# The inverse roots of the query and key norms: from GpSimd's power to ten Vector operations in PSUM

## The reference, cut to what matters

```
for i in range(6):
    x = attn_layer(shift_tokens(x), ...) + x
    x = ffn_layer(shift_tokens(x), ...) + x

# in attn_layer: 16 heads of 64
q, k, v = split(x @ Wqkv, 3)
l2norm(t) = t / maximum(norm(t, axis=-1), 1e-12)
q = l2norm(q) * q_scale ; k = l2norm(k) * k_scale
q = q * cos * scale + rotate_half(q) * sin * scale      # k: 1 / scale
out = local_attention(q, k, v) @ Wo                     # windows of 32, each sees 64 keys
```

## Time and profile before

| | us |
|---|---|
| median of 3 runs | 4746.68 (4745.28 to 4752.33) |
| the profiled execution | 4743.42 |
| its span in the trace | 4741.6 |

### The profile page before, as it was taken

How to read it: one execution, slowest core, us unless ns; L and a number is a source line. 1 busy time by engine, 2 the same in 40 slices (tenths; PEclk the granted TensorE clock), 3 DMA queues, 4 the chain that set the end, 5 groups by cost and what they waited for, 6 DMA issues and landing times. The chain is left out here.

```text
span 4741.6 us, 161504 instructions
## 1 busy us (share of the span) xinstructions
PE 4145.7 (87%) x67078; PEld 2784.5 (59%) x67078; DVE 2917.3 (62%) x4217; ACT 2627.4 (55%) x4417; POOL 3317.3 (70%) x1514
## 2 busy tenths in 40 slices
PE   5878788779999999999999999999999999999994
PEld 2434344356666666666666666666666666666663
DVE  5565656556666666666666666666666666666664
ACT  2535354446556556666556555656566555655562
POOL 0000000189889888988888889988898888888891
PEclk8989888899999999999999999999999999999997
DMA  0000000112222222222222222222222222222222
GB/s 27 2 15 2 15 16 2 41 45 56 65 70 74 54 69 65 71 56 65 65 69 63 56 65 73 75 51 69 65 72 57 62 65 69 63 56 65 69 73 71
DMA packets 284546, 258.84 MB, mean 55 GB/s; under 512 B 122871, under 2 KB 258508, under 8 KB 271148
## 3 DMA queue, kind: packets, MB, share of 16 engines
q1 hardware_dynamic: 283820, 248.14, 19.5%
HBM read 117.63 MB, written 29.77 MB: 31 GB/s over the span
## 5 line engine op out<-in xcount | busy, mean ns | idle before, releaser
L783 DVE TENSOR_TENSOR products<-bank_d,table 128x1024 f32<-128x1024 f32 x772 | 937.9, 1215 | 722.5 <-ACT sq L610 696.5
L908 POOL TENSOR_TENSOR rnorm<-clamped,minus_half 128x32 f32<-128x32 f32 x192 | 1044.0, 5438 | 16.0
L903 POOL TENSOR_TENSOR products<-products 128x2048 f32<-128x2048 f32 x192 | 870.7, 4535 | 152.0 <-DVE products L783 152.0
L409 PE MATMUL bank_d<-w_qkv,xT 128*128 128x512 f32 x1544 | 806.4, 625 | 19.6 <-DVE products L783 14.7
L610 ACT ACTIVATE sq<-bank_d 128x512 f32<-128x512 f32 x772 | 467.9, 606 | 478.7 <-PE bank_d L409 468.6
L926 POOL TENSOR_TENSOR qk_rot<-products,rnorm 128x2048 f32<-128x2048 f32 x192 | 695.5, 3622 | 14.9 <-POOL rnorm L908 14.5
L870 POOL MEMSET ident<- 128x128 f32 x1 | 0.2, 205 | 917.1 <-POOLq L1044 917.1
L781 DVE TENSOR_REDUCE ss<-sq 128x16 f32<-128x1024 f32 x386 | 468.6, 1214 | 232.5 <-ACT sq L610 232.5
L933 POOL TENSOR_TENSOR prob<-prob,inv_sum 128x1024 f32<-128x1024 f32 x192 | 365.1, 1901 | 187.5 <-DVE inv_sum L763 187.5
L1471 DVE TENSOR_REDUCE part_max<-s_max 128x1 f32<-128x512 f32 (+3 forms) x768 | 398.5, 554 | 151.2 <-PE s_max L1220 100.5
L455 PE MATMUL bank_a<-ident,qk_rot 128*128 128x128 f32 x3072 | 414.7, 291 | 76.8 <-issue 64.7
(11 more groups left out here) (158 smaller groups left out, 7216.9 us busy)
## 6 DMA issues: line engine op xcount, KB each, us to landing
v_back<-v SPq DMA_DIRECT2D x96, 768.0 KB, 5.4
w_qkv<-in_Wqkv_dram SPq DMA_DIRECT2D x25, 1024.0 KB, 5.1
v_back<-v SPq DMA_DIRECT2D x192, 128.0 KB, 5.4
w_qkv<-in_Wqkv_dram SPq DMA_DIRECT2D x25, 512.0 KB, 5.4
xs<-x_layers SPq DMA_DIRECT2D x194, 64.0 KB, 2.1
w_o<-in_Wo_dram SPq DMA_DIRECT2D x24, 512.0 KB, 5.5
xr<-x_layers SPq DMA_DIRECT2D x96, 128.0 KB, 2.2
x<-x SPq DMA_DIRECT2D x96, 128.0 KB, 1.8
```

The lines of the kernel that those rows point to most:

```text
L409: nc.tensor.matmul(bank[:, :], xT[:, P * a:P * (a + 1)], w_qkv[:, col:col + 512], start=True, stop=True).then_inc(d_filled if i < 8 else a ...
L783: nc.vector.tensor_tensor(products[:, a, head:head + 8, :, :].rearrange("p h r (o d) -> p h r o d", o=2), bank[:, :].rearrange("p (h r d) ...
L903: link(nc.gpsimd.tensor_tensor(products[:, a, :, 0, :], products[:, a, :, 0, :], products[:, a, :, 1, :], ALU.add))
L908: link(nc.gpsimd.tensor_tensor(rnorm[:, a, :], clamped[:, a, :], minus_half[:, :], ALU.pow))
```

## The change

`inverse_norms` leaves POOL. DVE computes the 32 inverse roots of a half right behind the product of that half's last chunk (chunk 3 and chunk 7): the clamped sum of squares, a first guess by integer arithmetic on the bits, one cubic correction, one Newton step. Nine linked operations and a last one, each 128x32. Their intermediate values x, t, u lie in the PSUM bank of that last product, so the bank is freed (`d_free`) by the last root and not by the product. The product counts in a new semaphore, `products_ready`, on which POOL's `add_products` starts; `norm_qk` now waits on `d_free` for the roots.

```diff
--- before.py
+++ after.py
@@ -168,8 +168,9 @@
 
         ss = sb("ss", [P, 2, 2 * HEADS])
         rnorm = sb("rnorm", [P, 2, 2 * HEADS])
-        clamped = sb("clamped", [P, 2, 2 * HEADS])
-        minus_half = sb("minus_half", [P, 2 * HEADS])
+        root_y = sb("root_y", [P, 2 * HEADS])
+        root_u = sb("root_u", [P, 2 * HEADS])
+        minus_half = sb("minus_half", [P, 2])
         epsilon = sb("epsilon", [P, 2])
         var_eps = sb("var_eps", [P, 2])
         rstd = sb("rstd", [P, 2])
@@ -222,6 +223,7 @@
         a_filled, a_free = sem("a_filled"), sem("a_free")
         squared = sem("squared")
         var_ready = sem("var_ready")
+        products_ready = sem("products_ready")
         qk_ready = sem("qk_ready")
         table_ready = sem("table_ready")
         scores_ready, scores_used = sem("scores_ready"), sem("scores_used")
@@ -780,11 +782,32 @@
                 if c:
                     nc.vector.tensor_reduce(ss[:, a, HEADS * kq:HEADS * (kq + 1)], sq[i // 2 % 2][:, :, :], AX.X, ALU.add)
                 head = HEADS * kq + 8 * c
-                nc.vector.tensor_tensor(
+                product = nc.vector.tensor_tensor(
                     products[:, a, head:head + 8, :, :].rearrange("p h r (o d) -> p h r o d", o=2),
                     bank[:, :].rearrange("p (h r d) -> p h r d", r=2, d=DH // 2).unsqueeze(3).to_broadcast([P, 8, 2, 2, DH // 2]),
                     t4[:, kq, :, :].rearrange("p (r o) d -> p r o d", o=2).unsqueeze(1).to_broadcast([P, 8, 2, 2, DH // 2]),
-                    ALU.mult).then_inc(d_free, 1)
+                    ALU.mult)
+                if i % 4 == 3:
+                    product.then_inc(products_ready, 1)
+                    dve.wait_ge(products_ready, 2 * pair.n + a + 1)
+                    inverse_norms(a, bank).then_inc(d_free, 1)
+                else:
+                    product.then_inc(d_free, 1)
+
+            def inverse_norms(a, bank):
+
+                x, t, u = (bank[:, 2 * HEADS * k:2 * HEADS * (k + 1)] for k in range(3))
+                y, w = root_y[:, :], root_u[:, :]
+                link(nc.vector.tensor_scalar(x, ss[:, a, :], FLT_MAX, 1e-24, ALU.min, ALU.max))
+                link(nc.vector.tensor_scalar(y.bitcast(i32), x.bitcast(i32), -0.5, float(RSQRT_MAGIC), ALU.mult, ALU.add))
+                link(nc.vector.tensor_tensor(t, x, y, ALU.mult))
+                link(nc.vector.tensor_tensor(t, t, y, ALU.mult))
+                link(nc.vector.tensor_scalar(w, t, 0.375, -1.25, ALU.mult, ALU.add))
+                link(nc.vector.tensor_tensor(u, t, w, ALU.mult))
+                link(nc.vector.scalar_tensor_tensor(y, u, 1.875, y, ALU.add, ALU.mult))
+                link(nc.vector.tensor_tensor(t, x, y, ALU.mult))
+                link(nc.vector.scalar_tensor_tensor(t, t, -0.5, y, ALU.mult, ALU.mult))
+                return nc.vector.scalar_tensor_tensor(rnorm[:, a, :], t, 1.5, y, ALU.add, ALU.mult)
 
             def variances(s):
 
@@ -902,17 +925,12 @@
             def add_products(s, a):
                 link(nc.gpsimd.tensor_tensor(products[:, a, :, 0, :], products[:, a, :, 0, :], products[:, a, :, 1, :], ALU.add))
 
-            def inverse_norms(a):
-
-                link(nc.gpsimd.tensor_scalar(clamped[:, a, :], ss[:, a, :], FLT_MAX, 1e-24, ALU.min, ALU.max))
-                link(nc.gpsimd.tensor_tensor(rnorm[:, a, :], clamped[:, a, :], minus_half[:, :], ALU.pow))
-
             def normalise_x1(pair):
 
                 pool.wait_ge(var_ready, pair.n + 1)
                 link(nc.gpsimd.tensor_tensor(var_eps[:, :], mean_var[:, :, 1], epsilon[:, :], ALU.add))
                 nc.gpsimd.tensor_scalar(neg_mean[:, :], mean_var[:, :, 0], -1.0, 1.0, ALU.mult, ALU.mult)
-                link(nc.gpsimd.tensor_tensor(rstd[:, :], var_eps[:, :], minus_half[:, 0:2], ALU.pow))
+                link(nc.gpsimd.tensor_tensor(rstd[:, :], var_eps[:, :], minus_half[:, :], ALU.pow))
                 for a in range(2):
                     last = nc.gpsimd.tensor_scalar(xn[:, a, :], xs1[pair.par][:, a, :], neg_mean[:, a:a + 1],
                                                    rstd[:, a:a + 1], ALU.add, ALU.mult)
@@ -923,6 +941,7 @@
                 back1 = s.pair(1)
                 if runs(back1):
                     pool.wait_ge(a_filled, ring_a.at(s, f"qk{4 * a + 3}")[1] + 1)
+                pool.wait_ge(d_free, chunk_at(s.pair(0), 4 * a + 3)[1] + 1)
                 nc.gpsimd.tensor_tensor(qk_rot[:, a, :].rearrange("p (h d) -> p h d", d=DH),
                                         products[:, a, :, 0, :],
                                         rnorm[:, a, 0:2 * HEADS].unsqueeze(2).to_broadcast([P, 2 * HEADS, DH]),
@@ -937,9 +956,8 @@
             def step(s):
                 now, back1, back3 = s.pair(0), s.pair(1), s.pair(3)
                 if runs(now):
-                    pool.wait_ge(d_free, chunk_at(now, 3)[1] + 1)
+                    pool.wait_ge(products_ready, 2 * now.n + 1)
                     add_products(s, 0)
-                    inverse_norms(0)
                 if runs(back3):
                     normalise_x1(back3)
                 if runs(back1):
@@ -949,11 +967,10 @@
                 if runs(back1):
                     normalise(back1, 1)
                 if runs(now):
-                    pool.wait_ge(d_free, chunk_at(now, 7)[1] + 1)
+                    pool.wait_ge(products_ready, 2 * now.n + 2)
                     if s.p == POS - 1:
                         make_table(s.f + 1)
                     add_products(s, 1)
-                    inverse_norms(1)
                     norm_qk(s, 1)
                 if s.p == POS - 1:
                     nc.gpsimd.sem_clear(p_link)
```

## The result

| kernel | median us | from, to | runs |
|---|---|---|---|
| before | 4746.28 | 4745.28, 4752.33 | 4 |
| changed | 5028.69 | 5012.24, 5044.53 | 4 |

The ratio is 1.059, 95% interval 1.056 to 1.063: slower by 282 us, where 201 were forecast. The profiled execution took 5022.58 us, its span 5020.8.

A forecast was written before the change was run, and what follows sets the result against it. POOL was taken as the nearer bound, PE 1.1 us a step behind. Three steps of 2.21 us plus one of 1.76 make 8.39 us a round, 201 us over 24 rounds; on 4743.4 us that gives 4945 us, range 4850 to 5040.

The forecast's parts named there:

- C: Time by which each chain of ten root operations delays everything behind it on DVE: 2.35 us, from 2.0 to 2.95.
- The rival of dear PSUM: Root operations on DVE cost more in PSUM, 2.95 us a chain: 5046 us in all; chance 7%.
- Second chain: Half 1's roots behind chunk 7's product delay row_sum(1), POOL's normalise(1) and PE's transposes; 0.93 us is covered.
- First chain: Half 0's roots behind chunk 3's product hold the bank PE needs for chunk 5; scores come 0.79 us later.
- Wait of the second transposes: PE's second probability transposes wait 1.3 us or more for POOL's prob, itself released by inv_sum.
- Sum per step: Both chains' delay to a step: 2.21 us in p = 1 to 3, 1.76 us in p = 0 behind the loop's jump.
- The rest costs nothing: add_products starts as early as before, norm_qk's wait is met, and p = 3's rotary tables fit POOL's free time.
- The faster rival: The second chain vanishes in slack and only PE's lost xn wait shows, 109 us: 4635 us; chance 7%.
- The first chain costs nothing: PE's chunk 5 does not set the scores, so p = 1 to 3 cost 1.42 us each: 4888 us; chance 10%.
- no change: DVE's delay and PE's lost xn wait cancel, which takes a chain of 1.15 us; chance 3%.
- What was to be seen: POOL busy some 570 of 1000 us, DVE 365 us busier, steps of 39.3 us in p = 1 to 3.
- The clock falls at the new waits: Each new PE wait lowers its clock, at 1.6 us each adding 154 us: 5099 us; chance 4%.

The follow-up runs named there:

- half1_on_dve: The changed kernel with only half 1's roots on DVE; half 0 keeps its power on POOL. 5094.2 us, ratio 1.075 to the kernel before.
- after_late_v: The changed kernel with the v_back transfers within SBUF issued only after the last attnT copy: 4958.0 us, ratio 1.046 to the kernel before.
- half0_in_gap: The kernel before with only half 0's power moved to DVE, behind the product of chunk 6, ahead of the gap before row_sum 0: 4726.4 us, ratio 0.996.
- before_early_v: The kernel before with SP's v_back transfer block moved ahead of its x block: 4945.2 us, ratio 1.043.
- idle_reduces: The kernel before with 20 unused 128x32 reductions in SBUF added per step on DVE behind x1: 4756.8 us, ratio 1.003.

## Why the prediction came out as it did

The direction and the two places of the loss on DVE were right, and they bring 170 to 180 of the 201 us forecast. 282 us were measured. That this lies inside the range is in part luck: the range went that high for dear operations in PSUM, which did not come. What filled it is a loss of some 105 us that the prediction didn't have. Step by step:

- **C = 2.35 us.** Measured 2.29. The operations stand 0.22 to 0.24 us apart and the register wait leaves almost nothing. PSUM as source or target costs under 10 ns: the groups of the root operations have 195 to 199 ns with a result in PSUM and 191 to 192 with one in SBUF. The rival of dear PSUM is out. The Trainium skill ("VectorE: DVE Perf Modes", section on the TRN2 errata) gives 120 cycles for a PSUM source against 58, by estimate 65 ns more; this trace does not agree: the operation that reads ss from SBUF (L801) takes 0.20 us, the one that reads the bank (L805) 0.19.
- **Second chain, C - 0.93 = 1.42 us.** Measured alone 1.30 (half1_on_dve). Right, and it is the larger part of the 1.78 us.
- **First chain, chunk 5 held 1.08 us, 0.79 in the scores.** The mechanism was right ("if chunk 5 isn't held" did not happen), the size not: the wait is 0.67 us and the chain adds 0.48. PE takes the bank 0.05 us after the last root, not 0.23 as I had set, and arrives a little later itself. In exchange a wait came that I had not named: scores 1 wait 0.52 us for DVE's prob. It lies ahead of T, where the wait for POOL's prob ends last, so it should cost nothing; that is argued, not tested.
- **Wait of the second transposes, 1.3 us or more.** 1.44. The chain POOL prob from inv_sum from the roots is as put.
- **Sum per step, 2.21 us and 1.76 at the jump.** 1.78 us undisturbed, and 2.2 at the jump (45.00 us against 42.80 in the mean of 22), where 1.76 had been put. The first chain is hidden there, as said: chunk 5 starts at 2247.96 without a wait. The second costs C - 0.59 = 1.70 with the measured C. The rest stands just ahead of the jump, where chunk 3 of the next pair waits 0.98 us in the mean (0.52 before); the profile names DVE's product, but in the round shown that ended at 2236.28 and PE goes on at 2236.94, 1.4 us behind a packet of q8, and with v_back late (after_late_v) the wait is gone in all 22 rounds. So it looks like the same late supply. 72 x 1.78 + 24 x 2.2 = 181 us: the steps came out smaller than put and the jump larger, so part of the nearness to 201 is two errors that cancel. The comparison with v_back late on both sides gives 171 to 177.
- **What the sum did not hold.** PE's gaps in the probabilities by v, 67.8 - 2.5 = 65 us, and what follows them. In the 22 rounds of the table above the change costs 271 us: 166 by the 1.78 and 2.2 us, and 105 in the steps with a gap, of which the gaps are 63. The other 42 stand behind the gaps; a lowered clock is part of it (it follows 18 of the 37 gaps of the whole trace), and how much was not separated. The step that failed is "The rest costs nothing": it named semaphores and POOL's table, and not SP. I had followed DVE's delay to row_sum and to PE, but not PE's delay to the DMA queue. A later PE lets SP's order run ahead of it, and the same 1 MB then stands ahead of the next packet of q8.
- **The faster rival, 4635 us.** Its mechanism can be had (half0_in_gap), but its price was wrong. The 96 x 1.13 = 109 us were named as the most that the change can give back, and the rival used them as the outcome. Under the xn wait lies another chain, by the lines ACT's, which leaves 0.27 us in an undisturbed step, 19 us in 72 of them; the steps with the jump gain nothing (43.0 us against 42.8). 20 were measured.
- **The other rivals.** "The first chain costs nothing" is out, chunk 5 is held; "no change" is out with the measured C.
- **A slip in reading.** PE's 38.8 us at the jump are the total of 13 waits, 3 us a round, not 38.8 "once a round". Nothing in the sum rests on it.
- **What was to be seen.** POOL's 570 us in 1000 came as 556 and DVE's 365 more as 353; steps of 39.3 us as 38.93, but only where no issue gap falls into them.
- **The clock falls at the new waits.** Not so: the mean is 0.98 from 2000 to 3000 us, and the undisturbed steps, each with a wait of 1.4 us, last 38.93 us again and again. It falls behind half of the issue gaps. The stretches of 2270 to 2277, 2280 to 2283 and 2283 to 2290 us, as in the earlier trace rows:

```profile
2270.00:2277.00 7.00, 6.53 (x172) 4.57 (x174) 0.51 (x1) 3.86 (x8) 6.75 (x2) 1.00 0.62 163
2280.00:2283.00 3.00, 3.00 (x36) 1.81 (x29) 0.00 (x0) 1.42 (x3) 0.00 (x0) 0.52 0.02 5
2283.00:2290.00 7.00, 7.00 (x44) 5.24 (x42) 4.99 (x11) 5.13 (x12) 1.61 (x1) 0.96 0.00 0
```

After the gap of 1.56 us that ends at 2279.20 the granted clock is 0.52 for 3 us, about the lower of the two levels, 1.2 GHz, and 0.96 again behind them. The DMA share ahead of it is 0.62, most of it v_back.

The runs show that the time of v_back decides whether there is a gap (both ways, by SP's list alone), and the traces that a packet of instructions is late in each of them. The Trainium skill ("Runtime: NRT & Kernel Launch", Instruction fetch mechanics) says that an engine's sequencer loads the next block of its instructions by a DMA queue of its own while it executes, and that this is mostly hidden. The trace agrees that there are such queues (q8 moves 9.52 MB in 581 packets in both kernels); it does not agree that it stays hidden beside v_back. That q8 is PE's own queue is inferred, from PE going on 1.2 to 1.8 us behind its packet every time. What stays open is what holds the packet back: the trace shows when it starts, not when it was asked for, so that it queues behind the data of q1 is the likeliest reading and not shown.

## What to carry to other kernels

Where an operation moves onto an engine in order, its place is worth more than its price: the same 192 chains cost 282, 41 or 12 us by place and by the transfers around them. Put it in front of a real gap, and in a bank that no one is waiting for. When a change makes one engine late, list what now goes out early against it, bulk DMA above all. Look in the timeline for idle time that no engine releases, and in the DMA view for the packets of the instruction queues around it.

## What was unexpected of the hardware

- Bulk transfers within SBUF issued 1.1 us earlier relative to PE made the kernel 4.3% slower, with every computing engine's list unchanged (before_early_v, in which x, xs and w_o also go out later). PE's gaps were 1.3 to 2.7 us each, each behind a late packet of q8, and a stretch at half clock can follow.
- Twenty more operations a step on DVE brought the packets of q14 from 145 to 256; ten more (half1_on_dve) brought 146. With the 256 came an issue gap on DVE at every jump of the loop, of 5.1 us where a chain stands right ahead of the jump and of 0.7 to 2.8 us elsewhere. The Trainium skill ("Runtime: NRT & Kernel Launch", Instruction fetch mechanics) says that a taken branch out of the loaded window forces a load; the number of packets fits, 111 more in 24 rounds. In idle_reduces, with a gap of 0.7 us, the price was 0.3%; the price of the 5 us was not separated.
- Linked operations of 128x32 on DVE follow each other at 0.22 to 0.24 us in the changed kernel, whether they read and write PSUM or SBUF; in SBUF before it was 0.21 to 0.23.
